# Normalising attention probabilities on GpSimd: one multiply per head in place of one per unit

## The reference

```
# light: windows of 128 tokens, 8 heads of 64
attn = softmax(einsum('bwhid,bwhjd->bwhij', q, k)); out = attn @ v; out @ wo
# route: 50 rounds of coordinate descent on the scores, then the best 128 tokens
# heavy: 128 chosen queries, 256 keys, 8 heads of 64
attn = softmax(einsum('bhid,bhjd->bhij', q, k)); out = attn @ v; out @ wo; scatter to the chosen rows
```

## Time and profile before

| | |
|---|---|
| three runs | 500.12 to 501.89 us, median 501.69 |
| the profiled execution | 501.88 us, its span 500.1 |
| mean granted TensorE clock | 0.986 of full speed |
| busy: PE / DVE / ACT / POOL | 447.7 / 346.6 / 346.5 / 263.8 us |

### The profile page before, as it was taken

How to read it: one execution, slowest core, us unless ns; L and a number is a source line. 1 busy time by engine, 2 the same in 40 slices (tenths; PEclk the granted TensorE clock), 3 DMA queues, 4 the chain that set the end, 5 groups by cost and what they waited for, 6 DMA issues and landing times.

```text
span 500.1 us, 11927 instructions
## 1 busy us (share of the span) xinstructions
PE 447.7 (90%) x4021; PEld 390.7 (78%) x4021; DVE 346.6 (69%) x1130; ACT 346.5 (69%) x1260; POOL 263.8 (53%) x297
## 2 busy tenths in 40 slices
PE   3676888999899989988997989999999999999994
PEld 1464777888898977877886977889888889888883
DVE  6767788778788998789779984545546564556551
ACT  2268898778798868857776757767666777667761
POOL 7316566375566676331333334554555666655655
PEclk9999999999999999989999889999999999999998
DMA  8860000000001010000000000100010000110002
GB/s 223 252 263 23 13 11 12 12 23 23 12 22 32 5 32 23 22 12 2 12 13 10 12 2 18 33 17 7 11 18 13 12 12 11 17 18 11 7 7 21
DMA packets 18107, 16.26 MB, mean 33 GB/s; under 512 B 1952, under 2 KB 16816, under 8 KB 17792
## 3 DMA queue, kind: packets, MB, share of 16 engines
q1 hardware_dynamic: 14048, 11.70, 7.4%
q0 software_dynamic: 3248, 3.41, 4.2%
q10 hardware_dynamic: 752, 0.40, 0.3%
HBM read 10.23 MB, written 5.28 MB: 31 GB/s over the span
## 4 chain that ended last, share of the span: by engine, by line
PE 49%; DVE 11%; POOL 4%; issue 4%; ACT 3%; POOLq 0%; ACTq 0%; DVEq 0%
PE bank L872 6%; PE bank L883 5%; PE bank L898 5%; PE bank L780 4%; PE bank L639 4%; PE bank L641 4%; PE bank L640 4%; PE bank L810 4%; PE bank L839 3%; PE bank L910 3%; DVE cd_min L1182 2%; ACT pr L570 2%; PE bank L794 2%; POOL pr L399 2%; PE bank L821 2%
## 5 line engine op out<-in xcount | busy, mean ns | idle before, releaser
L399 POOL TENSOR_TENSOR pr<-pr,rinv 128x512 f32<-128x512 f32 x64 | 66.8, 1044 | 100.6 <-DVE rinv L1142 100.3
L411 POOL TENSOR_TENSOR pr<-pr,rinv 128x512 f32<-128x512 f32 x64 | 72.8, 1158 | 63.5 <-DVE rinv L1287 63.5
L570 ACT ACTIVATE pr<-bank,nmx 128x128 f32<-128x128 f32 x256 | 90.5, 378 | 20.1 <-DVE nmx L1136 20.1
L613 ACT ACTIVATE pr<-bank,nmx 128x256 f32<-128x256 f32 x128 | 59.5, 488 | 19.3 <-DVE nmx L1281 19.3
L1281 DVE TENSOR_REDUCE nmx<-bank 128x2 f32<-128x512 f32 x64 | 41.9, 682 | 35.0 <-PE bank L872 35.0
L623 ACT ACTIVATE pt<-bank 128x512 f32<-128x512 f32 x64 | 38.2, 597 | 27.5 <-PE bank L883 27.5
L570 ACT ACTIVATION_READ_ACCUMULATOR pr<-bank,nmx 128x1 f32 x256 | 55.8, 218 | 0.0
L794 PE MATMUL bank<-ident,pr 128*128 128x128 f32 x256 | 39.2, 275 | 11.6 <-POOL pr L399 9.8
L1136 DVE TENSOR_REDUCE nmx<-bank 128x4 f32<-128x512 f32 x64 | 42.3, 673 | 6.8 <-PE bank L780 6.6
L794 PEld LDWEIGHTS bank<-ident,pr 128*128 128x128 f32 x256 | 29.5, 140 | 17.8 <-POOL pr L399 12.4
L883 PE MATMUL bank<-ident,pr 128*128 128x128 f32 x256 | 38.9, 274 | 2.3 <-ACT pt L623 2.3
(11 more groups left out here) (222 smaller groups left out, 1318.7 us busy)
## 6 DMA issues: line engine op xcount, KB each, us to landing
mod_bc<-mod_rows_scratch SPq DMA_DIRECT2D x1, 3072.0 KB, 11.5
X<-in_L_attn_x SPq DMA_DIRECT2D x4, 512.0 KB, 9.0
xh_scratch<-xhs SPq DMA_DIRECT2D x16, 128.0 KB, 1.8
out<-X SPq DMA_DIRECT2D x16, 128.0 KB, 1.8
mod_bc<-mod_rows_scratch SPq DMA_DIRECT2D x1, 1024.0 KB, 4.5
wkv_raw<-in_L_ffn_wkv_light SPq DMA_DIRECT2D x1, 512.0 KB, 10.7
wmod_sb<-in_L_wmod ACTq DMA_DIRECT2D x1, 384.0 KB, 5.4
wq_raw<-in_L_ffn_wq_heavy POOLq DMA_DIRECT2D x1, 256.0 KB, 7.1
```

What stands on the lines that cost most here:

```text
L399: pool.tensor_tensor(q, q, rinv[u][:, :, None].broadcast_to([P, 4, P]), ALU.mult)\
L411: pool.tensor_tensor(q, q, rinv[u][:, 0:2, None].broadcast_to([P, 2, N]), ALU.mult)\
L570: act.activation(pr[u][:, i * P:(i + 1) * P], ps[bank][:, i * P:(i + 1) * P], ACT.Exp, bias=nmx[u][:, i:i + 1], accum_out=sums[u][:, i:i + ...
L613: act.activation(pr[u][:, i * N:(i + 1) * N], ps[bank][:, i * N:(i + 1) * N], ACT.Exp, bias=nmx[u][:, i:i + 1], accum_out=sums[u][:, i:i + ...
```

## The change

GpSimd multiplies each head by itself, with an instruction that takes one tensor and one column of numbers: four of 128x128 for a light unit, two of 128x256 for a heavy one. Each adds one to `pn`, and TensorE waits for four or two times the old count.

```diff
             def normalise(b, u):
                 g = 4 * b + u
                 pool.wait_ge(lt["ri"], g + 1)
-                q = pr[u][:, :].rearrange("p (h t) -> p h t", h=4)
-                pool.tensor_tensor(q, q, rinv[u][:, :, None].broadcast_to([P, 4, P]), ALU.mult)\
-                    .then_inc(lt["pn"], 1)
+                for i in range(4):
+                    q = pr[u][:, i * P:(i + 1) * P]
+                    pool.tensor_scalar(q, q, rinv[u][:, i:i + 1], None, ALU.mult).then_inc(lt["pn"], 1)
...
             def normalise_h(b, u):
                 g = 4 * b + u
                 pool.wait_ge(hv["ri"], g + 1)
-                q = pr[u][:, :].rearrange("p (h t) -> p h t", h=2)
-                pool.tensor_tensor(q, q, rinv[u][:, 0:2, None].broadcast_to([P, 2, N]), ALU.mult)\
-                    .then_inc(hv["pn"], 1)
+                for i in range(2):
+                    q = pr[u][:, i * N:(i + 1) * N]
+                    pool.tensor_scalar(q, q, rinv[u][:, i:i + 1], None, ALU.mult).then_inc(hv["pn"], 1)
...
             def p_transpose(b, u):
                 g = 4 * b + u
-                pe.wait_ge(lt["pn"], g + 1)
+                pe.wait_ge(lt["pn"], 4 * g + 4)
...
             def p_transpose_h(b, u):
                 g = 4 * b + u
-                pe.wait_ge(hv["pn"], g + 1)
+                pe.wait_ge(hv["pn"], 2 * g + 2)
```

## The result

The changed kernel takes 568.45 us (median of four runs, 564.02 to 571.24) against 501.79: a ratio of 1.133, 95% interval 1.124 to 1.141. The forecast was 502.5, the range ended at 509. The chance had been put at 0.35 on the right side, and the size was far out.

The account below looks back on a forecast made before the run. TensorE was taken as nearly full in the first and heavy attention stages, GpSimd counting only by latency. 501.88 + 1.8 (light units) - 1.0 (VectorE) = 502.7, adjusted by 0.19 to the median: 502.5 us, range 498.5 to 509.

Parts of the forecast that it names:

- price of a piece: GpSimd's time for one multiply by a column: 0.30 us light (unit +0.20), 0.465 us heavy (unit -0.07).
- dear end: Upper bound for a GpSimd piece, from the two-tensor multiply with a broadcast operand: 0.355 us light, 0.57 us heavy.
- slower rival: GpSimd pieces pay a second fixed part, 0.10 us, for fetching the column: light 0.455, heavy 0.67, total 519.7; chance 0.35.
- heavy margin: Heavy attention: fourth unit ready 0.71 us before TensorE takes it, so zero change unless a heavy piece exceeds 0.59 us.
- middle stage: Light attention beside the selection, 194 to 322 us: GpSimd's longer light units cost +1.8 us (-3.6 to +3.8).
- Nine exposed units: Of 64 light units, only nine, between 194 and 322 us, move TensorE one for one: nine x 0.20 = +1.8 us.
- zero before 194 us: Light attention mixed with the first attention: no TensorE wait on L399, GpSimd has 52 us free, so no change.
- VectorE held off: VectorE instructions wait out a whole GpSimd instruction; shorter pieces free four on the path: up to -2.0, taken as -1.0 us.
- the case that the prediction put at +1.0: Four VectorE routing products in a row, each held by another GpSimd piece: +1.0 us in place of -1.0.
- reading of the tail: End of the kernel: ScalarE's copies pace it, so a faster GpSimd gains zero; slower heavy units could cost +0.4 us.
- nine waits: TensorE's transposes L794 idle for GpSimd's `pr` nine times, 9.8 us together, read as each batch's fourth unit, 194 to 322 us.

Follow-up runs that it names:

- price list: Kernel before, with lists of four equal GpSimd instructions added behind its last scatter, to read the spacing of each kind; total time not compared.
- the constant: The changed kernel, each piece multiplying by the constant 0.125 in place of the column, without the division by the sum: 540.43 us, ratio 1.077.
- two-tensor per head: The change's pieces, waits and increments, but each piece a two-tensor multiply with the column repeated as second tensor: 503.74 us, ratio 1.0043.
- closed halves: Kernel before, light units cut into two two-tensor multiplies of 256 columns, TensorE's transposes still waiting for both: 500.84 us, ratio 0.9988.

## Why the prediction was wrong

**The step that failed is the price of a piece.** It was bounded by a fill and a two-tensor multiply, and "nearest" was a select at 0.25 us. The light piece is 0.58, outside both ends (0.15 and 0.355); the heavy piece 0.90 against a dear end of 0.57. The unspoken premise was that one tensor and a column can't cost more an element than two tensors. The price list says 2.5 against 1.66 ns. The fixed part is larger too, 0.26 us a piece by a column against 0.14. The select was near in shape and not in price; the fill and the copy, at 0.86 ns an element, say nothing of what another instruction costs.

**The slower rival had the right place and threshold, and half of the price.** It named a second fixed part, 0.10 us a piece over the dear end, for a trip to fetch the column. The fixed part grew by 0.26 - 0.14 = 0.12, of which the column itself is 0.07 to 0.09. What the rival lacked is the rate: 0.11 us more in a light piece and 0.22 in a heavy one. Its condition for the heavy stage, a piece above 0.59, was met, and with the measured unit its formula gives 16 x (4 x 0.81 - 0.71) = 40.5; the landmarks say 40.8, the run of the heavy part alone 40.3. With the constant (a unit of 1.63) it gives 29.0 against 28.4 by the landmarks, with one multiply a unit (1.55) 23.8 against 20.6. That the heavy margin is 0.71 us was read rightly from the earlier trace rows.

**The middle stage came out at its size by luck.** Nine exposed units x 1.34 are 12.1; between the landmarks 11.8 were lost in the changed kernel and 9.4 in the light part alone. But the second step that failed is the count: that only nine units move TensorE. These are TensorE's waits for normalised units in the kernel before (209.5 to 318.7 us), then in the changed one up to the selection (0 to 225.4) and between the landmarks (225.4 to 346.4):

```profile
PE bank L794 <- POOL pr L399: 9.1, 7, 2.7
...
PE bank L794 <- POOL pr L400: 14.4, 13, 2.7
...
PE bank L794 <- POOL pr L400: 20.9, 27, 2.4
```

Between the landmarks seven waits became 27, and their sum grew by 11.8, as much as the stretch. Of the 40 waits in all only 12 are for the fourth unit of a batch, 28 for the first three. The table below shows that the count stays near nine up to 1.55 us a unit (eleven in all) and rises beyond.

**The zero before 194 us fell with the size.** The prediction named its cover, 52 us of free GpSimd, and didn't work out how far it reaches. The runs give that (light unit from the spacing; lateness of the selection's start and of the stretch behind it, against 209.5 and 109.2; beside each, TensorE's waits for normalised units, in us and times):

| light unit, us | run | selection late by | waits up to it | stretch longer by | waits in it | nine units would give |
|---|---|---|---|---|---|---|
| 1.00 | before | 0 | 0.7, 2 | 0 | 9.1, 7 | 0 |
| 1.43 | two-tensor per head | -0.5 | 1.3, 2 | 1.4 | 11.7, 9 | 3.9 |
| 1.55 | one multiply a unit | -1.8 | 1.7, 2 | 4.0 | 12.4, 9 | 5.0 |
| 1.97 | constant | 4.4 | 6.7, 9 | 5.1 | 15.9, 21 | 8.7 |
| 2.34 | light part alone | 15.8 | 14.3, 14 | 9.4 | 21.2, 29 | 12.1 |
| 2.34 | the change | 15.9 | 14.4, 13 | 11.8 | 20.9, 27 | 12.1 |

Up to about 1.5 us a unit costs nothing up to the selection; behind that the loss runs away, and TensorE's waits there grow by 13.7 of the 15.9. Why units come late there is read from the windows and waits of the changed kernel and was not tested by itself: GpSimd is busy 122.62 of 149 us, and others that need it queue behind the units. The first row is the window, the next two are VectorE's wait for the residual, after and before.

```profile
60.00:209.00 149.00, 128.80 (x1147) 112.57 (x1146) 111.86 (x429) 111.46 (x457) 122.62 (x196) 0.99 0.05 16
...
DVE st L1067 <- POOL X L360: 7.7, 8, 2.5
...
DVE st L1067 <- POOL X L360: 1.8, 4, 0.8
```

VectorE's statistics waited 1.8 us for the residual L360 before, and 7.7 now. So GpSimd, which the prediction called free in throughput, had become more than four fifths full in that stretch, with its order of steps fixed; the count of exposed units could not see that.

**VectorE held off** was read rightly in the kernel before, but shorter pieces by themselves free little of it. In that kernel every routing product that took over 0.32 us, fifteen of them, ended 0.14 to 0.15 us behind a two-tensor instruction of GpSimd. Shorter two-tensor pieces gain the products little: their mean is 390 ns with pieces of one head and 420 with halves, against 411 before, because products in a row are each held by another piece, the case that the prediction put at +1.0: with pieces of one head 25 products take over 0.32 us. The mean falls where the operation changes, also where one multiply by a column takes a whole unit; the groups are those of the closed halves, of one multiply a unit and of the change:

```profile
L1097 DVE CUSTOM_DVE_ANT_0 rprod<-h,tok_bc 128x128 f32<-128x128 f32 x64 | 23.4, 420 | 0.1
...
L1094 DVE CUSTOM_DVE_ANT_0 rprod<-h,tok_bc 128x128 f32<-128x128 f32 x64 | 19.4, 357 | 0.1
...
L1096 DVE CUSTOM_DVE_ANT_0 rprod<-h,tok_bc 128x128 f32<-128x128 f32 x64 | 18.2, 337 | 3.5 <-POOL h L378 3.3
```

With one multiply a unit `cd_t` starts 0.02 us behind the start of a unit, as it started 0.04 behind one in the earlier trace rows, but ends 0.74 before that unit does:

```profile
223.06 1.56 POOL L399 TENSOR_SCALAR pr<-pr,rinv 128x512 f32<-128x512 f32 x1
...
223.08 0.80 DVE L1187 TENSOR_SCALAR cd_t<-s_rows,cd_c 32x256 f32<-32x256 f32 x1
```

In the change the products beside a piece end 0.09 to 0.10 us ahead of it, while `cd_t` still ends 0.14 behind one. So beside the multiply by a column the hold can end early; it isn't the shorter piece alone that frees VectorE. `sel` takes 0.47 us in the change in place of 1.18:

```profile
L1213 DVE TENSOR_TENSOR sel<-score,w1m 32x256 f32<-32x256 f32 x1 | 0.5, 473 | 0.0
```

What that is worth in time was not measured by itself; the selection that starts 1.8 us early with one multiply a unit, and the gap to the nine units in the table, would fit it. The reading of the tail, that ScalarE's copies pace it, had no run of its own.

Two readings of rows were off, and no term hangs on them: the heavy units of the earlier trace rows have a mean of 1.16 us and not 1.04, as the fourth of a batch takes 1.61, and the first of the nine waits in the earlier trace rows is for the second unit of its batch and not the fourth.

Two sections of a page of the Trainium skill bear on this. GPSIMD Engine Reference, section 4.1 (Engine selection), holds operations with one input to run at about line rate; the copy takes 0.86 ns an element and the multiply by a constant, which also reads one tensor, 2.49, so for the multiply the measurement decides. Section 7 of the same page (Performance pitfalls for Q7 kernels) gives some 102 cycles for a read command that doesn't overlap with the one before; as an estimate at the page's 1.2 GHz that is 0.085 us. The column's 0.07 to 0.09 over a constant is of that size; that the column is a read command of its own is not shown.

## What to carry to other kernels

An operation that isn't in the trace has no price until it is timed by itself; here it lay outside the bracket made of a fill, a select and a two-tensor multiply on the same engine, and a list of four in a row at two sizes settles it in one run. Try an operation both whole and in pieces: here the operation alone cost 24 us and the split alone 2, and together they cost 66.7. When a step gets longer, look for two limits: the margin of each consumer, read from when a unit is ready and when it is taken, and the point at which the engine itself fills up, behind which the loss grows faster than the step. Where a consumer takes a unit block by block, opening it in parts may be worth a little; here the kernels with halves or heads opened were 0.3 to 0.5% faster than the one before.

## What the runs showed of the hardware that was not expected

On GpSimd a multiply of a 128-row tile by a scalar costs about 2.5 ns an element, whether the scalar is a constant or a column (the fixed part of the spacing is 0.49 - 0.32 = 0.17 and 0.58 - 0.32 = 0.26); by a second tensor, repeated or full, 1.66 ns; a copy 0.86. Four two-tensor pieces in a row occupy 1.43 us where one whole multiply takes 1.00, so an instruction more costs some 0.14 us, as much as the prediction read from two sizes. By a column a further instruction costs 0.26 us.

A VectorE instruction that started beside a two-tensor multiply of 1.04 us on GpSimd ended 0.14 us behind it; beside a multiply by a column of 1.56 us the same instruction ended 0.74 us before the multiply did. In that run ten routing products lie wholly inside such a multiply and take no more than 0.32 us; in the kernel before none does.
